# Query and key stacks with dimensions seven partitions apart, 112 contraction rows, rows of 8 KB and no memsets

## The chip, the cores and the metric

The kernel runs on one core of a Trainium2 chip. The metric is the device time of one execution in microseconds. The profile is one such execution.

## The reference, cut to what matters

Eight batches of `x` (256 channels by 512 positions) go through four layers: masked cross attention with 16 heads of 16 dimensions, a ternary-weight gated layer, a long convolution and an fp8 layer. The change touches the first one only:

```python
q = einsum('oc,bct->bot', Wq, layernorm(x)) + bq      # b, 256, 512
k = einsum('oc,bcs->bos', Wk, ctx) + bk
q, k, v = (t.reshape(b, 16, 16, 512) for t in (q, k, v))   # b, head, dim, position
dot = einsum('bhdt,bhds->bhts', q, k) / sqrt(16)
mask = target_mask[:, :, :, None] * source_mask[:, :, None, :]
dot = mask * dot - (1.0 - mask) * 1e6
amap = softmax(dot, axis=-1) * mask
out = einsum('bhts,bhds->bhdt', amap, v)
x = x + tanh(g_xattn[0]) * out
```

## The kernel before

**Projection** (`phase_project`, from about 0 to 133 us of the span). For each batch it computes q and k in fp32 and splits each into three bf16 parts (a value, the rest, the rest of that). They go to DRAM as `q_parts` and `k_parts`, shape (batch, part, 256 channels, 512). SyncE (SP) issues every DMA of the kernel, in program order; the three stores of a part tensor stand at L183. GpSimd also builds `rows8`, the mask rows, which SP stores once at L227 and L228 as `mask_q` and `mask_k`, 8 rows of 512 for each batch.

**Attention** (`phase_attention`, about 137 to 605 us) works on 16 units of 8 heads, two for each batch, u = 2b + h. For a unit SP fills one slot of `q_stack` and one of `k_stack` (four slots each, L530 and L536, in `load_unit`). A slot has 128 partitions by 8 heads by 512 positions of bf16. Its partitions are the contraction rows of a matmul. Six blocks of 16 partitions each hold the 16 dimensions of one part of q beside one part of k (`Q_PART`, `K_PART`), so that one bf16 matmul sums the six products that make an fp32-like score. Partitions 96 to 101 are mask rows and 102 and 103 hold the negated row maxima (`place_max`, L550, from `mrow`). Partitions 104 to 127 are zeroed once at the start (L621, L622 on GpSimd, L836, L837 on VectorE). In DRAM a head's 16 dimensions are adjacent channels, so a partition of a block, one dimension of 8 heads, is read as 8 rows of 1 KB.

The work on TensorE (PE) for each unit goes in 8 steps k. Each step has 4 score matmuls (L749, into `ps_s`), 4 matmuls for the maxima of later units (`max_tile`, L728, into `ps_m`, reduced by VectorE at L814) and 4 matmuls of probabilities with values (L759). ScalarE takes the exponentials (L696). The maxima run ahead: in steps 0 to 3 of unit u the second half of the tiles of unit u+1, from step 4 on the first half of unit u+2. Before that first tile of unit u+2 PE waits for all 14 DMAs of its slot (`qk_loaded`, L788). In step 4 PE also transposes the maxima (`turn_max`, L737), ScalarE copies them to `mrow` in step 5 (L674), and SP writes them into the stack (L550).

SP's order in a unit: `load_unit` for unit u+2 (14 DMAs), `gather_den` for unit u-1 (L565, L566 to DRAM, a wait until they have landed, L568 back, L571), in every other unit `load_batch`, `store_inv` (L577), `place_max` for u+1 (L550, waits for `mrow`), `spread_inv` (L583), weights (L545). Then the next unit's `load_unit`. The slot that it fills was freed long before, so its start is set by SP's order.

Of the kernel before, what the change touches and what calls it, by code (L numbers as in the profile page):

```python
# [6 lines left out]
BF16 = mybir.dt.bfloat16  # L7
# [4 lines left out]
P = 128  # L12
B = 8
C = 256
L = 512
CT = C // P
LT = L // P
ROWT = B * CT
HEADS, HD = 16, 16
UH = 8  # L20
# [7 lines left out]
BLOCKS = len(Q_PART)  # L28
MASK_ROW = BLOCKS * HD
MAX_ROW = MASK_ROW + BLOCKS  # L30
EXTRA = BLOCKS + 2


# [59 lines left out]
def phase_project(core, ctx, A):  # L93
# [4 lines left out]
    nc, X = core.nc, core.X  # L98
    RING = 3
    with ExitStack() as free:  # L100
# [9 lines left out]
        rows8 = sb("rows8", [B, 2, EXTRA, L], BF16)  # L110
# [7 lines left out]
        f = sb("qk_f", [P, 2, 2, CT, L], F32)  # L118
        r = sb("qk_r", [P, 2, 2, CT, L], F32)
# [12 lines left out]
        split_step, rows_ready, rows_stored = sem("split_step"), sem("rows_ready"), sem("rows_stored")  # L132
# [20 lines left out]
        with nc.Block() as block:  # L153

            @block.sync
            def _(sp):
# [59 lines left out]
                for b in range(B):  # L216
                    store_parts(b, KS)
                    if b + RING < B:
                        load_ctx(b + RING)
                    store_parts(b, QS)  # L220
                    if b + 2 < B:
                        load_mask(b + 2)
                        load_weights(b + 2)
                    store_values(b)
                    if b == 1:
                        sp.wait_ge(rows_ready, 2)
                        sp.dma_start(core.mask_q, rows8[:, 0]).then_inc(rows_stored, 16)  # L227
                        sp.dma_start(core.mask_k, rows8[:, 1]).then_inc(rows_stored, 16)  # L228
                sp.wait_ge(rows_stored, 32)
                for p in range(2):  # L230
# [219 lines left out]
def phase_attention(core, ctx, A):  # L450
# [6 lines left out]
    nc, X = core.nc, core.X  # L457
    DW = UH * L // P
    with ExitStack() as free:
# [13 lines left out]
        mrow = sb("mrow", [2 * UH, L], BF16)  # L473
# [5 lines left out]
        S = free.enter_context(nc.psum_tensor("ps_s", [P, 4, L], F32))  # L479
        M = free.enter_context(nc.psum_tensor("ps_m", [P, 3, L], F32))  # L480
# [5 lines left out]
        gate_ready, o_cleared = sem("gated_mask"), sem("o_cleared")  # L486
        zeroed = [sem(f"zeroed{i}") for i in range(4)]
# [22 lines left out]
        def bank(j):  # L510

            return (j if j < TURN_SLOT else j + 1) % 3
# [9 lines left out]
        with nc.Block() as block:  # L522

            @block.sync
            def _(sp):
                def load_unit(b, slot, h, fresh=False):
                    for blk in range(BLOCKS):
                        for dst, src, part in ((Q, core.q_parts, Q_PART[blk]), (K, core.k_parts, K_PART[blk])):
                            s = src[bass.ds(b, 1), part, h * P:(h + 1) * P, :]
                            sp.dma_start(dst[blk * HD:(blk + 1) * HD, slot],  # L530
                                         s.rearrange("a (h d) l -> d (a h) l", d=HD)).then_inc(qk_loaded[slot], 16)
                    if fresh:
                        sp.wait_ge(zeroed[slot], 2)
                    for dst, src in ((Q, core.mask_q), (K, core.mask_k)):
                        s = src[bass.ds(b, 1)].rearrange("a r l -> r a l").to_broadcast([EXTRA, UH, L])
                        sp.dma_start(dst[MASK_ROW:MASK_ROW + EXTRA, slot], s).then_inc(qk_loaded[slot], 16)  # L536

# [10 lines left out]
                def place_max(v, slot, h):  # L548
                    sp.wait_ge(mrow_ready, v + 1)
                    sp.dma_start(Q[MAX_ROW:MAX_ROW + 2, slot], mrow[:]).then_inc(m_placed[h], 16)  # L550

                load_unit(0, 0, 0, fresh=True)
                load_unit(0, 1, 1, fresh=True)
                load_batch(0, 0)
                load_weights(0, 0)
                load_weights(1, 1)
                sp.wait_ge(zeroed[2], 2)
                sp.wait_ge(zeroed[3], 2)
                place_max(0, 0, 0)
# [59 lines left out]
            def _(pool):  # L619
                for slot in (1, 3):  # L620
                    nc.gpsimd.memset(Q[96:P, slot], 0.0).then_inc(zeroed[slot], 1)  # L621
                    nc.gpsimd.memset(K[96:P, slot], 0.0).then_inc(zeroed[slot], 1)  # L622
                pool.wait_ge(zeroed[1], 2)
                pool.wait_ge(zeroed[3], 2)

                def batch(b, par, first, last):
# [90 lines left out]
            def _(pe):  # L717
                def max_tile(v, slot, tile, j):

                    hd, tc = tile // LT, tile % LT  # L720
                    n = TILES * v + tile
                    if j == TURN_SLOT + 2:
                        pe.wait_ge(mrow_ready, v)
                    elif TURN_SLOT <= j < TURN_SLOT + 2:
                        pe.wait_ge(max_red, n - 1)
                    elif not (same(v, 0) and tile < 3):
                        pe.wait_ge(max_red, n - 2)
                    nc.tensor.matmul(M[:, bank(j), :], Q[:, slot, hd, tc * P:(tc + 1) * P], K[:, slot, hd, :],  # L728
                                     start=True, stop=True).then_inc(max_mm, 1)
# [81 lines left out]
            def _(dve):  # L811
# [956 lines left out]
def build(nc, A, out):  # L1768
    core = Core()
# [5 lines left out]
    core.inv_rows = nc.dram_tensor("inv_rows", (2, UH, L), F32, kind="Internal").ap()  # L1775
    core.mask_q = nc.dram_tensor("mask_q", (B, EXTRA, L), BF16, kind="Internal").ap()
    core.mask_k = nc.dram_tensor("mask_k", (B, EXTRA, L), BF16, kind="Internal").ap()
    with ExitStack() as ctx:
# [10 lines left out]
        columns = sb("columns", [P, 16], F32)  # L1789
# [59 lines left out]
```

## Time and profile before

| | |
|---|---|
| median of 3 runs | 1348.16 us (1347.45 to 1355.43) |
| the profiled execution | 1347.74 us, span 1345.9 us |
| PE busy | 1115.3 us (83%) |
| VectorE busy | 1034.6 us (77%) |
| ScalarE busy | 667.1 us (50%) |
| GpSimd busy | 539.9 us (40%) |
| moved by DMA | 129.34 MB, mean 96 GB/s |
| attention, about 137 to 605 us | 468 us of the span |

The span is the profiled time from the first to the last instruction. PE is the busiest engine, but busy shares are means over four layers with different limits. What decides for this change is which wait ends last in the attention. The profile's own groups name it: the largest idle time ahead of the `ps_m` matmuls ends with a DMA into `k_stack`.

### The profile page before, as it was taken

Reading aid. Unit: us, or ns where it says so; the run is one execution under the profiler, and the core shown is the slowest. Engines: PE = TensorE matmul, PEld = TensorE weight load, DVE = VectorE, ACT = ScalarE, POOL = GpSimd, SP = SyncE. Lnnn points to the kernel's source line nnn. Section 1 sums busy time; section 2 is a strip of 40 time slices with the busy share of each in tenths; the row PEclk is TensorE's granted clock in tenths of the full one; section 3 lists DMA queues with packets and bytes.
Section 4 is the critical chain, followed back from the end, with each engine's and each line's share of the span. In section 5 each row is a group of like instructions: output and inputs, shape, how many; then the busy total and the mean of one; then the engine's idle time right before and its main releaser. Section 6 shows DMA issues by size and latency. Waiting matters only on the chain. (4 is left out here: it accounts for less than half of the span.)

```text
span 1345.9 us, 16068 instructions
## 1 busy us (share of the span) xinstructions
PE 1115.3 (83%) x4802; PEld 445.5 (33%) x4802; DVE 1034.6 (77%) x1564; ACT 667.1 (50%) x783; POOL 539.9 (40%) x407
## 2 busy tenths in 40 slices
PE   4985399978988899982899996699999999269676
PEld 2543022222222222211444443344444443134232
DVE  5787698866877787713999995588888887767898
ACT  1655057755767676781566664111000000486896
POOL 5766421423344234442011101587888886000021
PEclk8997679998999999996999999899999999589889
DMA  8798967765677656414111010111111110000011
GB/s 310 260 338 301 132 113 136 115 116 94 145 129 115 118 117 135 100 47 169 48 47 47 31 47 7 45 63 57 55 61 62 63 63 31 1 0 0 0 63 63
DMA packets 84275, 129.34 MB, mean 96 GB/s; under 512 B 13544, under 2 KB 53864, under 8 KB 83696
## 3 DMA queue, kind: packets, MB, share of 16 engines
q1 hardware_dynamic: 84224, 128.72, 39.2%
q8 instruction: 25, 0.41, 0.1%
q14 instruction: 26, 0.21, 0.1%
HBM read 104.44 MB, written 21.89 MB: 94 GB/s over the span
## 5 line engine op out<-in xcount | busy, mean ns | idle before, releaser
L814 DVE TENSOR_REDUCE mneg<-ps_m 128x1 f32<-128x512 f32 x512 | 321.9, 682 | 91.5 <-PE ps_m L728 90.8
L1358 PE MATMUL ps_y<-kv,toeplitz_sb 128*128 128x512 f32 x640 | 279.4, 595 | 10.0 <-POOL kv L1270 10.0
L696 ACT ACTIVATE probs<-ps_s 128x1024 f32<-128x1024 f32 x256 | 250.0, 1023 | 52.5 <-PE ps_s L749 52.3
L728 PE MATMUL ps_m<-k_stack,q_stack 128*128 128x512 bf16 x512 | 187.0, 406 | 59.3 <-DMA k_stack<-mask_k 55.3
L1358 PEld LDWEIGHTS ps_y<-kv,toeplitz_sb 128*128 128x128 f32 x640 | 121.0, 191 | 156.3 <-issue 156.3
L749 PE MATMUL ps_s<-q_stack,k_stack 128*128 128x512 bf16 x512 | 155.7, 388 | 11.7 <-ACT probs L696 11.2
L759 PE MATMUL ps_o<-probs,v_all 128*17 128x512 f32 x1024 | 139.5, 618 | 0.4 <-ACT probs L696 0.4
L1270 POOL TENSOR_TENSOR kv<-vT,ctxT_sb 128x2048 f32<-128x2048 f32 x32 | 118.7, 3710 | 39.1 <-PE ps_y L1358 32.4
L993 PE MATMUL ps_g<-w,xT_f 128*128 128x512 bf16 x512 | 120.1, 383 | 7.0 <-DVE h_f L1140 6.3
L644 POOL TENSOR_TENSOR inv_all<-inv_all,mb_b 128x512 f32<-128x512 f32 x16 | 20.4, 1274 | 252.2 <-DMA inv_all<-inv_rows 252.2
L1424 DVE TENSOR_TENSOR z<-ps_y,ctxT_sb 128x1024 f32<-128x1024 f32 x64 | 77.9, 1217 | 47.1 <-PE ps_y L1358 47.1
L728 PEld LDWEIGHTS ps_m<-k_stack,q_stack 128*128 128x128 bf16 x512 | 42.2, 99 | 217.0 <-DVE mneg L814 102.2
L1323 ACT ACTIVATE w_anchor<-w_f 128x512 f32<-128x512 f32 x32 | 20.1, 628 | 180.6 <-DMA w_f<-in_w 180.6
L1175 POOL TENSOR_TENSOR X<-X,down_sums 128x512 f32 (+1 forms) x16 | 20.5, 1283 | 195.6 <-ACT down_sums L1036 195.6
L1681 PE MATMUL ps_fp<-w 128*128 128x512 bf16 x256 | 66.3, 413 | 22.9 <-DVE w L1748 12.3
L1432 DVE TENSOR_REDUCE vT<-z 128x256 f32<-128x2304 f32 x32 | 81.7, 2553 | 1.1
L54 DVE BATCH_NORM_STATS2 bn<-X 128x6 f32<-128x512 f32 (+1 forms) x64 | 42.6, 683 | 46.9 <-POOL X L652 21.2
L749 PEld LDWEIGHTS ps_s<-q_stack,k_stack 128*128 128x128 bf16 x512 | 45.8, 98 | 81.6 <-ACT probs L696 34.3
L1048 ACT ACTIVATE sg_f<-ps_g,sc_f 128x512 f32<-128x512 f32 x64 | 42.7, 686 | 57.0 <-PE ps_g L993 37.7
L662 POOL TENSOR_SCALAR w<-w_sweep 128x512 bf16<-128x512 f32 x48 | 70.4, 1489 | 1.3
L993 PEld LDWEIGHTS ps_g<-w,xT_f 128*128 128x128 bf16 x512 | 48.4, 99 | 65.1 <-DVE h_f L1140 10.2
L980 PE MATMUL ps_d<-w,hT_f 128*128 128x512 bf16 x256 | 59.5, 387 | 1.6 <-ACT hT_f L1021 1.6
(163 smaller groups left out, 1649.7 us busy)
## 6 DMA issues: line engine op xcount, KB each, us to landing
w_sweep<-in_w SPq DMA_DIRECT2D x8, 1536.0 KB, 10.1
q_stack<-q_parts SPq DMA_DIRECT2D x96, 128.0 KB
k_stack<-k_parts SPq DMA_DIRECT2D x96, 128.0 KB
w_sweep<-in_w SPq DMA_DIRECT2D x16, 768.0 KB, 6.3
w_sweep<-in_w SPq DMA_DIRECT2D x16, 512.0 KB, 3.4
toeplitz_sb<-in_toeplitz SPq DMA_DIRECT2D x32, 256.0 KB, 2.6
w_f<-in_w SPq DMA_DIRECT2D x32, 256.0 KB, 2.9
k_parts<-qk_part SPq DMA_DIRECT2D x24, 256.0 KB, 7.5
```

The source lines that it names most:

```text
L662: nc.gpsimd.tensor_scalar(core.w3[:, m].rearrange("p a b -> p (a b)")[:, u * L:(u + 1) * L], wc[:, h, m, :], MAGIC, None, ALU.subtract).th ...
L696: nc.scalar.activation(pr[:, k % 2, 2 * slot:2 * slot + 2, :], S[:, 2 * slot:2 * slot + 2, :], ACT.Exp).then_inc(exp_done, 1)
L728: nc.tensor.matmul(M[:, bank(j), :], Q[:, slot, hd, tc * P:(tc + 1) * P], K[:, slot, hd, :], start=True, stop=True).then_inc(max_mm, 1)
L749: mm = nc.tensor.matmul(S[:, g, :], K[:, slot4, hd, (k % LT) * P:(k % LT + 1) * P], Q[:, slot4, hd, :], start=True, stop=True)
L759: mm = nc.tensor.matmul(O[32 * g:32 * g + HD + 1, :], V[:, par, sc, h * UH + 2 * g + G, :], pr[:, k % 2, g, :], start=(sc == 0), stop=(sc ...
L814: nc.vector.tensor_reduce(mneg[:, h, tile % LT, tile // LT:tile // LT + 1], M[:, bank(j), :], AX.X, ALU.max, negate=True).then_inc(max_red, 1)
L993: mm = nc.tensor.matmul(G[:, c % 2, j, :], xT[:, par, k, :], wt[:, k, c * L:(c + 1) * L], start=(k == 0), stop=(k == LT - 1))
L1270: nc.gpsimd.tensor_tensor(kv[:, g % 2].rearrange("p l (b j i) -> p (l b) j i", b=B, j=GROUP), over_j(group(vT, g)), over_i(group(cT, g)), ...
L1358: mm = nc.tensor.matmul(Y[:, q % 3, l2, :], T[:, g % 2, (lt - m) * P:(lt - m + 1) * P], kv[:, g % 2, m, :], start=(m == 0), stop=(m == lt))
L1424: nc.vector.tensor_tensor(z[:, g % 2, NB // 2 * half:NB // 2 * (half + 1), :, 0:GROUP], Y[:, q % 3].rearrange("p l (b j i) -> p (l b) j i" ...
L1432: nc.vector.tensor_reduce(group(vT, g), z[:, g % 2], AX.X, ALU.add).then_inc(red_ready, 1)
L1681: mm = nc.tensor.matmul(D[:, r, :], h8[:, j % 4, L * t + r * P:L * t + (r + 1) * P], proj[:, ot, :], start=(i == 0 and t == 0), stop=(i == ...
```

## The change

The partitions of a slot are laid out anew. Block j of dimension d stands at partition 7d + j instead of 16j + d, for j from 0 to 5, and partition 7d + 6 holds row d of the mask rows. That makes 112 rows (`ROWS`), all of them written by DMA, so the eight memsets and their semaphores go, and every matmul on the stacks reads partitions 0 to 111. The mask tensors in DRAM get 16 rows for each batch instead of 8. Rows 8 to 15 are written from the two constant rows of `rows8` (0 on the query side, 1 on the key side), so their products are 0. The maxima go to partitions 48 and 55. On the host the columns of `Wq` and `Wk` and both biases are permuted within each 128 channels from (head, dimension) to (dimension, head). A partition's 8 heads are then adjacent rows in DRAM and are read as one row of 8 KB. The order in which each engine issues is as before.

```diff
-MASK_ROW = BLOCKS * HD
-MAX_ROW = MASK_ROW + BLOCKS
+STEP = BLOCKS + 1
+ROWS = STEP * HD
 EXTRA = BLOCKS + 2
+MAX_ROW = STEP * BLOCKS + BLOCKS
...
-                        sp.dma_start(core.mask_q, rows8[:, 0]).then_inc(rows_stored, 16)
-                        sp.dma_start(core.mask_k, rows8[:, 1]).then_inc(rows_stored, 16)
+                        for side, dst in ((0, core.mask_q), (1, core.mask_k)):
+                            sp.dma_start(dst[:, 0:EXTRA], rows8[:, side]).then_inc(rows_stored, 16)
+                            for e in range(EXTRA, HD, 2):
+                                sp.dma_start(dst[:, e:e + 2], rows8[:, side, BLOCKS:EXTRA]).then_inc(rows_stored, 16)
...
-                            sp.dma_start(dst[blk * HD:(blk + 1) * HD, slot],
-                                         s.rearrange("a (h d) l -> d (a h) l", d=HD)).then_inc(qk_loaded[slot], 16)
-                    if fresh:
-                        sp.wait_ge(zeroed[slot], 2)
+                            sp.dma_start(dst[blk:ROWS:STEP, slot],
+                                         s.rearrange("a (d h) l -> d (a h) l", d=HD)).then_inc(qk_loaded[slot], 16)
                     for dst, src in ((Q, core.mask_q), (K, core.mask_k)):
-                        s = src[bass.ds(b, 1)].rearrange("a r l -> r a l").to_broadcast([EXTRA, UH, L])
-                        sp.dma_start(dst[MASK_ROW:MASK_ROW + EXTRA, slot], s).then_inc(qk_loaded[slot], 16)
+                        s = src[bass.ds(b, 1)].rearrange("a r l -> r a l").to_broadcast([HD, UH, L])
+                        sp.dma_start(dst[BLOCKS:ROWS:STEP, slot], s).then_inc(qk_loaded[slot], 16)
...
-                    sp.dma_start(Q[MAX_ROW:MAX_ROW + 2, slot], mrow[:]).then_inc(m_placed[h], 16)
+                    sp.dma_start(Q[MAX_ROW:MAX_ROW + STEP + 1:STEP, slot], mrow[:]).then_inc(m_placed[h], 16)
...
-                for slot in (1, 3):
-                    nc.gpsimd.memset(Q[96:P, slot], 0.0).then_inc(zeroed[slot], 1)
-                    nc.gpsimd.memset(K[96:P, slot], 0.0).then_inc(zeroed[slot], 1)
...
-                    nc.tensor.matmul(M[:, bank(j), :], Q[:, slot, hd, tc * P:(tc + 1) * P], K[:, slot, hd, :],
+                    nc.tensor.matmul(M[:, bank(j), :], Q[0:ROWS, slot, hd, tc * P:(tc + 1) * P],
+                                     K[0:ROWS, slot, hd, :],
...
-                        mm = nc.tensor.matmul(S[:, g, :], K[:, slot4, hd, (k % LT) * P:(k % LT + 1) * P],
-                                              Q[:, slot4, hd, :], start=True, stop=True)
+                        mm = nc.tensor.matmul(S[:, g, :], K[0:ROWS, slot4, hd, (k % LT) * P:(k % LT + 1) * P],
+                                              Q[0:ROWS, slot4, hd, :], start=True, stop=True)
...
-                for slot in (0, 2):
-                    nc.vector.memset(Q[96:P, slot], 0.0).then_inc(zeroed[slot], 1)
-                    nc.vector.memset(K[96:P, slot], 0.0).then_inc(zeroed[slot], 1)
...
+    def by_dim(v):
+        return np.ascontiguousarray(v.reshape(v.shape[:-1] + (CT, P // HD, HD)).swapaxes(-1, -2).reshape(v.shape))
```

SP at the end of one unit's load, before. The last number of a row is the shape that the DMA is issued with: partitions, rows for each, elements of a row.

```order
L530 DMA q_stack<-q_parts 16x8x512
L530 DMA k_stack<-k_parts 16x8x512
L536 DMA q_stack<-mask_q 8x8x512
L536 DMA k_stack<-mask_k 8x8x512
L539 DMA v_all<-v_rows 128x1088
```

The same place after the change.

```order
L532 DMA q_stack<-q_parts 16x4096
L532 DMA k_stack<-k_parts 16x4096
L536 DMA q_stack<-mask_q 16x8x512
L536 DMA k_stack<-mask_k 16x8x512
L539 DMA v_all<-v_rows 128x1088
```

A block's 8 rows of 512 elements for each partition have become one row of 4096 (8 KB). The mask rows stay rows of 1 KB and go to 16 partitions instead of 8. Nothing has changed places.

SP in the projection where the mask rows are stored, before.

```order
L189 DMA v_rows<-vp 128x1088 [waits v_ready]
L227 DMA mask_q<-rows 8x4096 [waits rows_ready]
L228 DMA mask_k<-rows 8x4096
L183 DMA k_parts<-qk_part 128x2x512 [waits p3_ready]
```

The same place after.

```order
L190 DMA v_rows<-vp 128x1088 [waits v_ready]
L229 DMA mask_q<-rows 8x4096 [waits rows_ready]
L231 DMA mask_q<-rows 8x1024 x4
L229 DMA mask_k<-rows 8x4096
L231 DMA mask_k<-rows 8x1024 x4
```

Eight small DMAs now stand between the values of batch 1 and the key parts of batch 2.

## Rows read from the trace of the kernel before

**Rows 1.** Waits in the attention: engine, line, releaser: us in total, times, longest.
```profile
PE ps_m L728 <- DMA k_stack<-mask_k: 55.3, 13, 21.7
PE ps_s L749 <- ACT probs L696: 11.2, 20, 1.1
PE ps_m L728 <- DVE mneg L814: 3.9, 15, 0.6
```

**Rows 2.** Timeline of the attention's start: start us, us, engine, instruction, idle before.
```profile
137.62 0.36 SPq L530 DMA_DIRECT2D q_stack<-q_parts  x1
142.28 0.43 SPq L530 DMA_DIRECT2D q_stack<-q_parts  x1
142.75 0.43 SPq L530 DMA_DIRECT2D k_stack<-k_parts  x1
140.25 1.76 DVE L837 MEMSET k_stack<- 32x2048 uint32 x1 [0.38 <-issue]
143.60 0.31 SPq L536 DMA_DIRECT2D k_stack<-mask_k  x1
154.12 2.00 PE L728 MATMUL ps_m<-k_stack,q_stack 128*128 128x512 bf16 x4 [21.65 <-DMA k_stack<-mask_k]
154.77 19.42 DVE L814 TENSOR_REDUCE mneg<-ps_m 128x1 f32<-128x512 f32 x32 [7.89 <-PE ps_m L728]
```

**Rows 3.** Busy time by stretch: A:B us, PE, PEld, DVE, ACT, POOL, PEclk, DMA share, GB/s.
```profile
148.50:154.10 5.60, 0.00 (x0) 0.00 (x0) 0.00 (x0) 0.00 (x0) 2.98 (x1) 0.50 1.13 128
258.50:265.00 6.50, 5.97 (x37) 1.69 (x34) 5.20 (x9) 5.90 (x8) 6.17 (x8) 1.00 1.13 125
160.00:166.00 6.00, 4.33 (x11) 0.97 (x11) 6.00 (x11) 0.00 (x0) 0.00 (x0) 0.91 1.13 117
40.00:70.00 30.00, 27.72 (x89) 16.45 (x87) 22.25 (x35) 20.74 (x31) 21.77 (x10) 1.00 0.90 303
```

**Rows 4.** DMA issues of the whole span: engine, count, KB each, median us to landing.
```profile
k_parts<-qk_part SPq DMA_DIRECT2D x24, 256.0 KB, 7.5
out<-X SPq DMA_DIRECT2D x16, 256.0 KB, 2.0
num<-odd_heads SPq DMA_DIRECT2D x64, 32.0 KB, 1.9
```

**Rows 5.** Timeline of PE at four units' first tiles, and the transposes behind two.
```profile
272.11 0.39 PE L728 MATMUL ps_m<-k_stack,q_stack 128*128 128x512 bf16 x1 [3.38 <-DMA k_stack<-mask_k]
302.35 0.61 PE L728 MATMUL ps_m<-k_stack,q_stack 128*128 128x512 bf16 x1 [6.29 <-DMA k_stack<-mask_k]
441.35 0.39 PE L728 MATMUL ps_m<-k_stack,q_stack 128*128 128x512 bf16 x1 [1.88 <-DMA k_stack<-mask_k]
443.83 0.39 PE L737 MATMUL ps_m<-ident,mm 128*16 128x128 bf16 x4
549.95 0.39 PE L728 MATMUL ps_m<-k_stack,q_stack 128*128 128x512 bf16 x1 [2.08 <-DMA k_stack<-mask_k]
554.02 0.39 PE L737 MATMUL ps_m<-ident,mm 128*16 128x128 bf16 x4
```

**Rows 6.** Busy time by stretch from one unit's first tile to the next's.
```profile
195.11:218.90 23.79, 23.25 (x133) 6.66 (x133) 20.45 (x34) 18.95 (x22) 4.78 (x4) 1.00 0.61 74
244.70:272.11 27.41, 23.48 (x133) 6.60 (x133) 21.28 (x36) 19.00 (x22) 11.05 (x10) 1.00 0.70 108
302.35:332.06 29.71, 25.82 (x132) 6.98 (x133) 21.42 (x36) 19.13 (x22) 11.05 (x10) 0.90 0.63 101
415.44:441.35 25.91, 23.48 (x133) 6.62 (x133) 21.28 (x36) 19.01 (x22) 11.05 (x10) 1.00 0.69 114
522.45:549.95 27.50, 24.88 (x133) 6.74 (x133) 21.26 (x36) 19.14 (x22) 11.06 (x10) 0.94 0.65 107
```

**Rows 7.** Timeline of SP in one unit.
```profile
259.38 0.54 SPq L565 DMA_DIRECT2D den_rows<-num  x1
272.35 0.36 SPq L568 DMA_DIRECT2D den<-den_rows  x1
277.09 0.70 SPq L550 DMA_DIRECT2D q_stack<-mrow  x1
282.33 0.33 SPq L530 DMA_DIRECT2D q_stack<-q_parts  x1
288.49 0.28 SPq L536 DMA_DIRECT2D k_stack<-mask_k  x1
```

**Rows 8.** Line 728: duration in ns min/median/max; then two score matmuls in the timeline.
```profile
L728 PEld LDWEIGHTS ps_m<-k_stack,q_stack x512: 95/98/152, 154.1 to 574.5; 128*128 128x128 bf16 x171
L728 PE MATMUL ps_m<-k_stack,q_stack x512: 379/379/634, 154.1 to 574.6; 128*128 128x512 bf16 x171
244.92 0.59 PE L749 MATMUL ps_s<-q_stack,k_stack 128*128 128x512 bf16 x2
```

**Rows 9.** Timeline of SP in the projection around the mask rows.
```profile
60.90 0.37 SPq L228 DMA_DIRECT2D mask_k<-rows  x1
62.09 1.82 SPq L183 DMA_DIRECT2D k_parts<-qk_part  x3
64.00 0.50 SPq L162 DMA_DIRECT2D cx<-in_ctx  x1
67.47 3.81 SPq L183 DMA_DIRECT2D q_parts<-qk_part  x3
```

More of the change, by code:

```diff
@@ L226, in _ @@
                         sp.wait_ge(rows_ready, 2)
-                        sp.dma_start(core.mask_q, rows8[:, 0]).then_inc(rows_stored, 16)
-                        sp.dma_start(core.mask_k, rows8[:, 1]).then_inc(rows_stored, 16)
-                sp.wait_ge(rows_stored, 32)
+                        for side, dst in ((0, core.mask_q), (1, core.mask_k)):
+                            sp.dma_start(dst[:, 0:EXTRA], rows8[:, side]).then_inc(rows_stored, 16)
+                            for e in range(EXTRA, HD, 2):
+                                sp.dma_start(dst[:, e:e + 2], rows8[:, side, BLOCKS:EXTRA]).then_inc(rows_stored, 16)
+                sp.wait_ge(rows_stored, 2 * 16 * (1 + (HD - EXTRA) // 2))
                 for p in range(2):
@@ L486, in phase_attention @@
         gate_ready, o_cleared = sem("gated_mask"), sem("o_cleared")
-        zeroed = [sem(f"zeroed{i}") for i in range(4)]
         qk_loaded = [sem(f"qk_loaded{i}") for i in range(4)]
@@ L525, in _, with load_unit @@
             def _(sp):
-                def load_unit(b, slot, h, fresh=False):
+                def load_unit(b, slot, h):
                     for blk in range(BLOCKS):
@@ L549, in place_max @@
                     sp.wait_ge(mrow_ready, v + 1)
-                    sp.dma_start(Q[MAX_ROW:MAX_ROW + 2, slot], mrow[:]).then_inc(m_placed[h], 16)
-                load_unit(0, 0, 0, fresh=True)
-                load_unit(0, 1, 1, fresh=True)
+                    sp.dma_start(Q[MAX_ROW:MAX_ROW + STEP + 1:STEP, slot], mrow[:]).then_inc(m_placed[h], 16)
+                load_unit(0, 0, 0)
+                load_unit(0, 1, 1)
                 load_batch(0, 0)
@@ L556, in _ @@
                 load_weights(1, 1)
-                sp.wait_ge(zeroed[2], 2)
-                sp.wait_ge(zeroed[3], 2)
                 place_max(0, 0, 0)
@@ L619, in _ @@
             def _(pool):
-                for slot in (1, 3):
-                    nc.gpsimd.memset(Q[96:P, slot], 0.0).then_inc(zeroed[slot], 1)
-                    nc.gpsimd.memset(K[96:P, slot], 0.0).then_inc(zeroed[slot], 1)
-                pool.wait_ge(zeroed[1], 2)
-                pool.wait_ge(zeroed[3], 2)
                 def batch(b, par, first, last):
@@ L1775, in build @@
     core.inv_rows = nc.dram_tensor("inv_rows", (2, UH, L), F32, kind="Internal").ap()
-    core.mask_q = nc.dram_tensor("mask_q", (B, EXTRA, L), BF16, kind="Internal").ap()
-    core.mask_k = nc.dram_tensor("mask_k", (B, EXTRA, L), BF16, kind="Internal").ap()
+    core.mask_q = nc.dram_tensor("mask_q", (B, HD, L), BF16, kind="Internal").ap()
+    core.mask_k = nc.dram_tensor("mask_k", (B, HD, L), BF16, kind="Internal").ap()
     with ExitStack() as ctx:
@@ L1830 @@
         "x": arr("x"), "ctx": arr("ctx_2048"), "mask": arr("mask_Bx1x2048_fk1"), "g_xattn": arr("g_xattn"),
-        "g_ffn": arr("g_ffn"), "bq": columns(inputs["L0_xattn_bq"]), "bk": columns(inputs["L0_xattn_bk"]),
+        "g_ffn": arr("g_ffn"), "bq": columns(by_dim(inputs["L0_xattn_bq"])), "bk": columns(by_dim(inputs["L0_xattn_bk"])),
         "mask_cols": np.ascontiguousarray(inputs["mask_Bx1x2048_fk1"].reshape(B, LT, P).transpose(2, 0, 1)),
         "bv": arr("L0_xattn_bv"),
-        "wqT": np.ascontiguousarray(inputs["L0_xattn_Wq"].T), "wkT": np.ascontiguousarray(inputs["L0_xattn_Wk"].T),
+        "wqT": by_dim(inputs["L0_xattn_Wq"].T), "wkT": by_dim(inputs["L0_xattn_Wk"].T),
         "wvT": np.ascontiguousarray(inputs["L0_xattn_Wv"].T),
```

## The prediction

> **What bounds the kernel now.** The list of waits, cut to the attention, comes first, because only the attention's loads change. PE's largest wait there is for the last DMA of a slot: 55.3 us in 13 waits, the longest 21.7 us [rows 1]. PE waits for ScalarE and VectorE 11.2 and 3.9 us. So the question is how long a unit's 14 load DMAs take, and what else hangs on them.
>
> The timeline of the start answers for the first unit. SP issues its first DMA at 137.62, the last (key mask rows) at 143.60 and is done with it at 143.91. PE starts at 154.12, 21.65 us idle, released by that load [rows 2]. The data is 10.2 us behind the issue. While it lands, the DMA engines show as fully busy but move only 128 GB/s; in a load inside the loop 125 GB/s; in the projection the same engines move 303 GB/s [rows 3]. A load is therefore limited by its own form. It has two features that the projection's traffic lacks: 16 adjacent partitions on the SBUF side, and rows of 1 KB on both sides. The rows alone are a weak reason: the projection's stores of `k_parts` are rows of 1 KB too (128x2x512), among the traffic at 303 GB/s.
>
> In the loop the same load ends PE's wait ahead of the first tile of unit u+2. Such waits are 3.38, 6.29, 1.88 and 2.08 us, for example [rows 5]; the 13 of the list less the first make 55.3 - 21.7 = 33.6 us. They cost more than that. The stretch from one unit's first tile to the next's is 27.41 us with a wait of 3.38 at its end, and 25.91 with 1.88: 24.03 us of work both times, at a granted clock of 1.00 [rows 5, 6]. But the stretch that begins behind the wait of 6.29 us has 0.90, and its PE work is 25.82 instead of 23.48 us [rows 6]: behind long waits the clock is at its lower level (1.2 of 2.4 GHz) for a few us.
>
> **The change part by part.**
>
> *Start.* One load is now 12 DMAs of 128 KB and 2 of 128 KB, 1.84 MB. At the 303 GB/s that the projection shows it would take 6.1 us; SP needs 143.91 - 137.62 = 6.3 us to issue it. I take the issue as the limit. Landing of the last one: about 2.3 us, beside 2.0 us for the stores of `out` (256 KB) and 1.9 for 32 KB, both in calm queues [rows 4]. PE starts at 143.9 + 2.3 = 146.2 instead of 154.12: **-7.9 us**. Everything behind it up to the loop is paced by VectorE's reductions (32 in 19.42 us [rows 2]) and moves along. The bounds are 0 (rate unchanged at 128 GB/s) and -10.2 (nothing behind the issue), some 1.5 us more if SP issues a DMA with fewer rows faster than the 0.47 us from one to the next [rows 2].
>
> The Trainium skill, SBUF — State Buffer, Door 1: The DMA port swizzle, says that the partition number decides which of 16 ports a transfer uses and that partitions 0 to 15 reach 4 of them, at about 104 GB/s; the trace agrees with its 125 to 128 GB/s, where two neighbouring loads overlap. By its formula partitions 7d + j reach 14 or 15 ports, none with more than two of the 16 rows. That rule would give 0.6 us for a DMA, 7.2 us for twelve, 0.9 us more than the issue, and the start would gain 7.0.
>
> *Loop.* From unit to unit the first tiles run from 195.11 to 549.95, 13 stretches in 354.84 us (first and last in [rows 6]). Without the load wait the first, 23.79 us, stays (it ends without one), and twelve take 24.03: 23.79 + 288.36 = 312.15. **-42.7 us**, of which some 33 are waits and some 9 clock. The clock's part rests on the stretches at 1.00, which have only short waits. After the last wait PE is slow once more: 554.02 - 549.95 = 4.07 us to the transposes against 443.83 - 441.35 = 2.48: **-1.6 us** [rows 5].
>
> This needs the load to be hidden in every unit. The worst case in the trace is the load whose first DMA was issued at 282.33 [rows 7]. PE wanted it at 302.35 - 6.29 = 296.06, 13.7 us later [rows 5]. The new load needs about 6.3 + 2.3 = 8.6, so 5.1 us of slack. It decides at (13.7 - 2.0) us for 1.84 MB, or 157 GB/s: above that no wait is left. The denominators profit too: they were issued at 259.38 behind the load and came back only at 272.35 [rows 7]; with the queues empty that is about 2 us instead of 12. So `place_max` will wait for `mrow` alone, and the next load starts no later than now relative to PE's steps.
>
> *Next limit.* With the loads away, PE is the bound at 23.48 of 24.03 us; VectorE has 21.28 and ScalarE 19.00 [rows 6].
>
> *Memsets.* Worth 0. VectorE's second one ends at 142.01, SP wants the mask rows of slot 0 only after 142.75 + 0.43 [rows 2]. Left in, they would still be hidden: the issue order is the same.
>
> *112 rows.* The number of columns is unchanged, and I take 0 for matmuls and weight loads. The trace has no matmul with fewer rows. See the third rival.
>
> *Mask rows.* Twice as many partitions, 8 rows of 1 KB each as before. I take them as 128 KB like a block in the 1.84 MB above. Its issue (0.31 us [rows 2]) may reach that of a block (0.43): 0.2 us at the start, within the landing estimate.
>
> *Projection.* SP has 8 more small DMAs of 16 KB, at 0.37 + 0.05 us each 3.4 us. SP is idle from 61.27 to 62.09 there and again from 64.50 to 67.47 [rows 9]. Key parts of batch 2 are stored 2.6 us later, the context of batch 5 is issued 2.6 us later, and the gap of 2.97 us ahead of the query parts takes it up. The 128 KB are 0.4 us at 303 GB/s in queues that are full. I take **+0.4**, bounds 0 and 3.4.
>
> **Sum.** -7.9 - 42.7 - 1.6 + 0.4 = -51.8 us. Against the profiled execution's 1347.74 that is 1296; the median of the runs, 1348.16, is 0.4 above it.
>
> **The rivals.**
>
> 1. *The load gets only somewhat faster* (chance 0.13), because 8 KB to a single partition, or DRAM, sets a rate between 128 and 157 GB/s, or because the mask rows land late. At 145 GB/s a load takes 12.7 + 2.0 = 14.7 us. The first unit starts at 137.62 + 14.7 = 152.3, 1.8 us earlier. In the worst units 1.0 us of wait is left, at most 12 us over all, so the loop gains 31 to 43: 1304 to 1316; nearer to 128 GB/s it reaches 1330. For it: each row still goes through one engine into one partition. Against it: the 303 GB/s that the same engines reach [rows 3].
>
> 2. *The loads are no faster* (0.07): their rate comes from something that both layouts share, such as 16 partitions for each DMA. Then the time stays near 1348, and the doubled mask bytes, 0.13 MB at 128 GB/s, add up to 1 us to each of 13 waits, 1361 at most. For it: the trace has no load of that size over spread partitions. Against it: fewer rows and more places to write leave no reason for the old rate that the rows show.
>
> 3. *112 rows make the weight load slow* (0.04), the case on the slower side. A weight load takes 98 ns and is hidden: two matmuls take 0.59 us, one 0.38, so they start 0.21 us apart [rows 8]. If fewer rows lost some fast form, nothing would show until the load exceeds 210 ns. Beyond that each ns counts for the 1,024 matmuls on the stacks: 50 ns more (260 ns in all) cost 51 us and eat the whole gain, 100 ns more cost 102 and give 1296 + 102 = 1398. The forecast turns into a loss from 260 ns on. The Trainium skill, TensorE: Matmul & The Clock Gate, Part 2, says that the load's time goes by columns and not by rows; no run here shows it yet, and by it this rival is void. A variant (0.02): the clock stays at its lower level because fewer rows count as less work. At 0.50 a unit's PE work nears twice 23.48 us, and 16 units make the time exceed 1600. Against it: at the start, with 11 matmuls in 6 us, the clock is already at 0.91 on average [rows 3].
>
> 4. *More than forecast* (0.04): issue and landing are both shorter and periods fall under 24.03 us, 1280 to 1286.
>
> **How the numbers follow.** Forecast 0.70 (1286 to 1304: the start's and the projection's bounds together). With the better half of rival 1, up to 1312, the range holds nearly 0.8. What a measurement of this kernel can tell from no change is 1%, 13.5 us. Faster by more: forecast 0.70, rival 1 0.13, rival 4 0.04, together 0.87. Within 1%: most of rival 2, 0.06. Slower: the rest of it, 0.01, and rival 3 with its variant, 0.06, together 0.07.
>
> **What would show it.** (a) PE's first `ps_m` matmul about 8.6 us behind SP's first stack DMA instead of 16.5. (b) No wait of PE on `k_stack` in the loop, all stretches from first tile to first tile near 24.0 us, granted clock 1.00. (c) About 10 us less between L565 and L568 on SP. (d) Weight loads of 98 ns and matmuls 0.21 us apart. (e) The projection's end within 0.5 us of now. It is wrong if stretches stay above 25 us, or if another wait stands where the load's did, such as for `mrow` in the stack.

## The result, and the profile after

The changed kernel takes 1309.63 us (median of 4 runs, 1308.91 to 1311.82), the kernel before 1349.37 in the same series (median of 4). The ratio is 0.970, interval 0.967 to 0.974: 39.7 us less, where 51.8 were forecast. The two profiled executions differ by 35.9 us (1347.74 and 1311.82; busy PE 1115.3 and 1114.2, moved 129.34 and 131.65 MB); the rest is the scatter of single executions. All accounts below are made between these two traces.

The page's row for the matmuls of the maxima, and the waits of the attention (137 to 605 us; total, times, longest). Line 720 is line 728 of before, 807 is 814.

```profile
L720 PE MATMUL ps_m<-k_stack,q_stack 112*128 112x512 bf16 x512 | 189.3, 410 | 26.9 <-DMA k_stack<-mask_k 16.1
```

```profile
PE ps_m L720 <- DMA k_stack<-mask_k: 16.1, 1, 16.1
DVE mneg L807 <- issue: 11.5, 4, 4.0
PE ps_m L720 <- DVE mneg L807: 10.8, 6, 3.3
```

Of the 13 waits for `k_stack` [rows 1] only the start's is left. One row is new: VectorE is idle for 11.5 us with nothing that the trace shows to wait for ("issue"). Another has grown: PE waits 10.8 us for the maxima, at most 3.3 at once, where it was 3.9 us, at most 0.6 [rows 1].

The start, from the timeline.

```profile
139.05 0.64 SPq L532 DMA_DIRECT2D q_stack<-q_parts  x1
139.75 0.57 SPq L532 DMA_DIRECT2D k_stack<-k_parts  x1
140.36 0.59 SPq L532 DMA_DIRECT2D q_stack<-q_parts  x1
...
147.36 0.60 SPq L536 DMA_DIRECT2D k_stack<-mask_k  x1
149.99 1.03 PE L720 MATMUL ps_m<-k_stack,q_stack 112*128 112x512 bf16 x2 [16.07 <-DMA k_stack<-mask_k]
```

PE starts 2.0 us behind the last issue's end (147.96), where it took 10.2 [rows 2]. But SP now needs 0.63 us from one issue to the next instead of 0.47, so the 14 of them need 8.9 us instead of 6.3.

Busy time by stretch (A:B us, PE, PEld, DVE, ACT, POOL, PEclk, DMA share, GB/s): five us in which only stack loads move, then four units, each from its transposes to the next unit's.

```profile
143.00:148.00 5.00, 0.00 (x0) 0.00 (x0) 0.00 (x0) 0.00 (x0) 0.00 (x0) 0.50 0.69 210
```

```profile
290.27:314.16 23.89, 23.20 (x132) 6.80 (x133) 20.96 (x37) 19.14 (x23) 11.05 (x10) 1.00 0.53 164
314.16:345.45 31.29, 26.09 (x132) 7.26 (x132) 21.19 (x37) 19.35 (x23) 10.04 (x9) 0.89 0.34 99
393.14:417.03 23.89, 23.20 (x133) 6.80 (x133) 20.96 (x37) 19.14 (x23) 11.05 (x10) 1.00 0.54 164
417.03:447.93 30.90, 26.02 (x133) 7.25 (x133) 21.19 (x37) 19.35 (x23) 10.05 (x9) 0.89 0.33 101
```

The rate is 210 GB/s where it was 128 [rows 3]. The DMA engines are busy for 0.69 of that time, and 128 KB every 0.63 us would be 208 GB/s, an estimate from the issues above. So SP's issue sets the rate here and no longer the load's form.

The units of the loop take 23.8 to 23.9 us at a clock of 1.00, as forecast, except two. Those two lose 31.29 + 30.90 - 2 x 23.89 = 14.4 us. They lie four units apart: units 2 to 13 run as a hardware loop of 3 iterations of 4 units, and the two places are its two turns. The timeline of VectorE and PE at the first turn:

```profile
328.24 0.69 DVE L807 TENSOR_REDUCE mneg<-ps_m 128x1 f32<-128x512 f32 x1 [4.03 <-issue]
328.99 0.39 PE L720 MATMUL ps_m<-k_stack,q_stack 112*128 112x512 bf16 x1 [3.28 <-DVE mneg L807]
330.82 2.48 DVE L807 TENSOR_REDUCE mneg<-ps_m 128x1 f32<-128x512 f32 x4 [1.89 <-issue]
331.57 0.61 PE L720 MATMUL ps_m<-k_stack,q_stack 112*128 112x512 bf16 x1 [1.76 <-DVE mneg L807]
331.97 1.06 PE L742 MATMUL ps_s<-q_stack,k_stack 112*128 112x512 bf16 x2
333.39 1.91 PE L752 MATMUL ps_o<-probs,v_all 128*17 128x512 f32 x8
```

VectorE stands still for 4.03 and 1.89 us, PE's next maxima matmul waits for it, and behind the pause PE runs at its lower clock level: the same 8 matmuls of line 752 take 1.05 us elsewhere (last fence of this section) and 1.91 here. So 5.9 us of standing still cost the unit 31.29 - 23.89 = 7.4 us.

The DMA view, attention only, has one more difference, on the queue named "instruction" (queue: packets, MB, share). Before:

```profile
q14 instruction: 10, 0.08, 0.1%
```

After:

```profile
q14 instruction: 20, 0.16, 0.1%
```

In the 15 us around the first turn, 320 to 335, the changed kernel has three packets of this queue:

```profile
q14 instruction: 3, 0.02, 0.6%
```

One of them is moved between 325 and 328 us, inside VectorE's first pause (324.2 to 328.2), and one between 328 and 331, which holds the second (328.9 to 330.8).

Other rows that answer to those of before. The denominators of one unit on SP (line 566 was 568), and the last matmul of the attention, which stood at 604.77:

```profile
233.36 0.58 SPq L563 DMA_DIRECT2D den_rows<-num  x1
233.98 0.55 SPq L564 DMA_DIRECT2D den_rows<-odd_heads  x1
235.72 0.33 SPq L566 DMA_DIRECT2D den<-den_rows  x1
```

```profile
568.76 1.05 PE L752 MATMUL ps_o<-probs,v_all 128*17 128x512 f32 x8
570.17 1.05 PE L752 MATMUL ps_o<-probs,v_all 128*17 128x512 f32 x8 [0.36 <-ACT probs L688]
```

### The profile page after: what moved, and what is told of

It is laid out like the page before. It is cut to its first block and busy times, and to the rows that moved or that the text cites. A ratio compares the mean times of both kernels' runs of the same rounds, so it can differ in the third digit from the quotient of the medians.

```text
span 1310.0 us, 16066 instructions
## 1 busy us (share of the span) xinstructions
PE 1114.2 (85%) x4802; PEld 449.6 (34%) x4802; DVE 1020.2 (78%) x1560; ACT 668.9 (51%) x783; POOL 525.9 (40%) x403
## 2 busy tenths in 40 slices
DMA packets 65213, 131.65 MB, mean 100 GB/s; under 512 B 13864, under 2 KB 31656, under 8 KB 61552
## 5 line engine op out<-in xcount | busy, mean ns | idle before, releaser
L720 PE MATMUL ps_m<-k_stack,q_stack 112*128 112x512 bf16 x512 | 189.3, 410 | 26.9 <-DMA k_stack<-mask_k 16.1
L742 PE MATMUL ps_s<-q_stack,k_stack 112*128 112x512 bf16 x512 | 155.2, 387 | 10.4 <-ACT probs L688 10.1
L752 PE MATMUL ps_o<-probs,v_all 128*17 128x512 f32 x1024 | 136.5, 605 | 0.4 <-ACT probs L688 0.4
L720 PEld LDWEIGHTS ps_m<-k_stack,q_stack 112*128 112x128 bf16 x512 | 43.5, 99 | 182.4 <-DVE mneg L807 99.1
L742 PEld LDWEIGHTS ps_s<-q_stack,k_stack 112*128 112x128 bf16 x512 | 46.6, 99 | 79.7 <-ACT probs L688 30.7
L1038 ACT ACTIVATE sg_f<-ps_g,sc_f 128x512 f32<-128x512 f32 x64 | 42.7, 686 | 57.1 <-PE ps_g L983 37.7
```

The costliest lines, as they stand in the source:

```text
L720: nc.tensor.matmul(M[:, bank(j), :], Q[0:ROWS, slot, hd, tc * P:(tc + 1) * P], K[0:ROWS, slot, hd, :], start=True, stop=True).then_inc(max ...
L742: mm = nc.tensor.matmul(S[:, g, :], K[0:ROWS, slot4, hd, (k % LT) * P:(k % LT + 1) * P], Q[0:ROWS, slot4, hd, :], start=True, stop=True)
L752: mm = nc.tensor.matmul(O[32 * g:32 * g + HD + 1, :], V[:, par, sc, h * UH + 2 * g + G, :], pr[:, k % 2, g, :], start=(sc == 0), stop=(sc ...
```

## Theories

The forecast treats placement (partitions 7 apart) and row size (8 KB) as one thing. Theory A: the rate comes from placement alone. Rival: from the longer rows. On the stalls, Theory F: at a loop's turn VectorE must fetch its instructions again, and whether it must depends on where the loop lies in its program, which the four missing memsets moved. Rivals: the 8 KB rows hold up that fetch; or the stall belongs to the new layout in some other way. The expectations give letters to these and other cases, and say beside each what it holds: B is row size as the cause of the rate; C, E and G are other causes of the stalls than the one under test; D is the first form of F, a fetch at the turn that the stack loads delay.

Every series had the kernel before in it, and each ratio is against that series: median 1352.66 us beside rows1, adj8, rows4 and unroll8, 1349.30 beside pad4, pad2, step2 and stores4, 1353.02 beside step2_m2, before_m2 and pad4_stores4. Differences in us between kernels of different series carry that scatter.

## Experiments on placement and row size

**rows1**: the changed kernel's partitions, the old rows of 1 KB. The host permutation goes.

```diff
-                            sp.dma_start(dst[blk:ROWS:STEP, slot],
-                                         s.rearrange("a (d h) l -> d (a h) l", d=HD)).then_inc(qk_loaded[slot], 16)
+                            sp.dma_start(dst[blk:ROWS:STEP, slot].rearrange("p (e r) l -> p e (r l)", r=1),
+                                         s.rearrange("a (e d r) l -> d (a e) (r l)", d=HD, r=1))
```

> The changed kernel with the host permutation and the load's source as before, so that every partition of a block is again read as 8 rows of 1 KB, while the partitions stay 7 apart. Theory A (16 adjacent partitions limit the old load, not the rows): the load stays fast; PE starts the attention within 1 us of the changed kernel's distance from SP's first stack DMA (10.9 us) or sooner, the loop keeps stretches of 23.9 us and no wait on the stack. SP issues a DMA each 0.47 us again (before: 0.47, changed kernel: 0.63). If the two stalls of 7 us at the loop's turns come from 8 KB rows ahead of instruction fetches, they vanish and the time is 1295 to 1300. Rival B (the rows of 1 KB limit it): the load moves 108 to 128 GB/s as before, the waits on the stack return, and the time is 1340 to 1350. Rival C (the stalls come from the new timing and not from the rows): fast load but stalls as in the changed kernel, 1307 to 1311.

Measured: 1308.42 us, 0.968 (0.962 to 0.974), as fast as the changed kernel. SP's issues are again 0.60 us long, PE starts 11.0 us behind the first. The two turns take 29.06 and 29.48 us. Rows of 1 KB are not what made the old loads slow. The stalls were to vanish if the 8 KB rows made them; they stayed, as rival C says.

**adj8**: the kernel before with the host permutation, so adjacent partitions and rows of 8 KB.

```diff
-                                         s.rearrange("a (h d) l -> d (a h) l", d=HD)).then_inc(qk_loaded[slot], 16)
+                                         s.rearrange("a (d h) l -> d (a h) l", d=HD)).then_inc(qk_loaded[slot], 16)
```

> The kernel before with only the host permutation and the load's source changed: rows of 8 KB to 16 adjacent partitions, memsets, 128 contraction rows and the mask rows as before. Theory A (adjacent partitions limit the load): the rate stays near 108 to 128 GB/s, the waits on the stack stay, 1340 to 1355. Rival B (row size): the loop's waits go, 1300 to 1315. SP's time for one issue tells whether 0.63 us belongs to the rows of 8 KB (then 0.63 here too) or to partitions that are not adjacent (then 0.47 here).

Measured: 1354.56 us, 1.002 (0.999 to 1.005). Its waits, the start of its SP timeline, and the stretch in which its first load lands:

```profile
PE ps_m L728 <- DMA k_stack<-mask_k: 59.2, 14, 22.4
```

```profile
138.42 0.41 SPq L530 DMA_DIRECT2D k_stack<-k_parts  x1
138.88 0.41 SPq L530 DMA_DIRECT2D q_stack<-q_parts  x1
```

```profile
148.50:154.10 5.60, 0.00 (x0) 0.00 (x0) 0.00 (x0) 0.00 (x0) 3.38 (x1) 0.50 1.04 117
```

8 KB rows into 16 adjacent partitions move 117 GB/s, no more than the 128 of before [rows 3]. And SP needs 0.46 us from one issue to the next: the longer issue belongs to the spread partitions, not to the rows. Both halves of the pair say the same, so Theory A stands.

**rows4**: rows of 4 KB, partitions 7 apart (in rows1's diff r is 4).

> The changed kernel with rows of 4 KB, two for each partition of a block (heads 0 to 3 and 4 to 7 apart in DRAM). If the stalls at the loop's turns grow with the row size, they are 7 us each in the changed kernel, 0 at 1 KB and between at 4 KB (about 3 us each), and the time is 1300 to 1306. If they depend on the timing alone they stay at 7 us: 1307 to 1311. SP's issue: 0.63 us if the number of rows has no part in it, less if it does.

Measured: 1308.49 us, 0.968 (0.962 to 0.974); the turns take 30.09 and 30.36 us. Over 1, 4 and 8 KB the stalls at a turn are 5.4, 6.3 and 7.2 us (means of two, over 23.89). But stores4 below has rows of 8 KB too, and its turns take 30.35 and 30.32 us, 6.4 over. Row size does not make the stalls; whether it changes their length, one trace for each kernel does not show.

**step2**: one edit of the kernel before. Blocks j and j+1 are interleaved over 32 partitions, each block on every second one; rows of 1 KB, 128 contraction rows and all memsets stay.

```diff
-                            sp.dma_start(dst[blk * HD:(blk + 1) * HD, slot],
+                            at = 2 * HD * (blk // 2) + blk % 2
+                            sp.dma_start(dst[at:at + 2 * HD:2, slot],
```

> The kernel before with one edit in the load: blocks j and j+1 share 32 partitions, every second one each (partitions 32 * (j // 2) + j % 2 + 2d), rows of 1 KB, memsets, 128 contraction rows, mask rows of 8 partitions and weights unpermuted as before. By the port rule such a block reaches 8 ports, and the load is limited by SP's issue (0.47 to 0.63 us for each DMA). Then the waits on the stack in the loop vanish or nearly so (the loads need more than 157 GB/s for that). Since VectorE's program is as before, theory F expects no stall at the loop's turns and thus 1294 to 1300, better than the changed kernel; rival G expects stalls and 1306 to 1311. If only a spread over the whole height helps, the waits stay and the time is 1340 to 1350.

Measured: 1295.87 us, 0.961 (0.957 to 0.966), 13.8 us less than the whole change. From its windows, its DMA view and its timeline:

```profile
138.00:143.00 5.00, 0.00 (x0) 0.00 (x0) 4.25 (x3) 0.00 (x0) 5.00 (x2) 0.50 0.65 206
```

```profile
q14 instruction: 10, 0.08, 0.1%
```

```profile
134.33 0.74 SPq L531 DMA_DIRECT2D q_stack<-q_parts  x1
...
142.72 0.31 SPq L537 DMA_DIRECT2D k_stack<-mask_k  x1
...
146.86 1.03 PE L729 MATMUL ps_m<-k_stack,q_stack 128*128 128x512 bf16 x2 [17.66 <-DMA k_stack<-mask_k]
```

Every second partition already gives 206 GB/s, again the rate of SP's issue, with the engines busy for 0.65 of the time. The start is 12.5 us behind the first issue, 1.6 more than 7 apart. SP's issues are done at 143.03, so it is the landing that takes 3.8 us instead of 2.0; that its mask rows still go to 8 adjacent partitions may be the reason, and was not tried. But no wait is left in the loop, there is no stall, and the mask stores are the old two. So 112 rows, 8 KB and a step of 7 are all unneeded for the loop; and the gain is larger where VectorE's program is left as it was.

## Experiments on the two stalls

**unroll8**: the changed kernel with the attention's hardware loop written out.

```diff
-            with eng.Fori(0, (B - 2) // 2) as i:
+            for i in range((B - 2) // 2):
```

> The changed kernel with the attention's hardware loop of three iterations written out for all engines; the same instructions in the same order, with no branch in the attention. Theory D (the two stalls of 7 us are instruction fetches at the loop's back-edge, late behind the stack loads): both vanish, each unit takes 23.9 us, and the time falls by 14 us to 1295. Rival E (something else at that place, such as a semaphore or a DMA of the kernel): the stalls stay and so does 1309.

Measured: 1298.39 us, 0.960 (0.954 to 0.966), 11.2 us less than the changed kernel where 14 were expected. The units at both places take 23.9 us and VectorE's "issue" row is gone. The instruction queue has 15 packets in the attention, whose program is now written out at full length, but none from 320 to 335. The stalls need the loop's turn.

**pad4**: the changed kernel with four memsets of one column of a spare tile on VectorE, where the four memsets of the stacks stood. They compute nothing.

```diff
+        spare = sb("spare", [P, 4], F32)
...
+                for i in range(4):
+                    nc.vector.memset(spare[:, i:i + 1], 0.0)
                 nc.vector.memset(O[:], 0.0).then_inc(o_cleared, 1)
```

> The changed kernel with four memsets of one column of a spare tile on VectorE where the four memsets of the stacks stood, so that VectorE's loop begins as many instructions into its program as in the kernel before. Everything else, also the timing of the loads, is as in the changed kernel. Theory F (the two stalls of 7 us are extra instruction fetches of VectorE, which the position of its loop in the program decides): no idle time of VectorE without a releaser at the loop's turns, about 10 instead of 20 packets on the small instruction queue in the attention, every unit 23.9 us, 1296 to 1299. Rival G (VectorE fetches at every turn in any layout, and the new timing only exposes it): stalls and packets as in the changed kernel, 1308 to 1311.

Measured: 1296.94 us, 0.962 (0.958 to 0.967), 12.7 us under the changed kernel. Three units over the first turn, and the packets:

```profile
288.50:312.38 23.88, 23.20 (x132) 6.79 (x132) 20.93 (x37) 19.14 (x23) 11.06 (x10) 1.00 0.57 164
312.38:336.27 23.89, 23.20 (x133) 6.79 (x133) 20.94 (x37) 19.15 (x23) 10.05 (x9) 1.00 0.43 129
336.27:360.15 23.88, 23.20 (x132) 6.79 (x132) 20.94 (x37) 19.14 (x23) 11.05 (x10) 1.00 0.54 163
```

```profile
q14 instruction: 11, 0.09, 0.1%
```

The unit over the turn takes 23.89 us instead of 31.29, and the packets are 11 instead of 20, with none from 320 to 335. Same layout, same rows: four instructions that do nothing take the stalls away.

**pad2**: the same with two.

> As pad4 with two memsets instead of four. Theory F: either as pad4 or as the changed kernel, nothing between (about 10 or 20 packets; 1297 or 1309). Rival G: 1309.

Measured (one run): 1312.86 us.

```profile
DVE mneg L808 <- issue: 12.8, 2, 6.5
```

```profile
q14 instruction: 20, 0.16, 0.1%
```

Two do not help; the pause changes its form (one of 6.5 us a turn instead of two, of 4.0 and 1.9).

**step2_m2**: the reversal. step2, with VectorE's four memsets written as two that clear the same bytes. SP's wait for the memsets of slot 2 goes too, so SP's program is one wait shorter.

```diff
-                sp.wait_ge(zeroed[2], 2)
...
-                for slot in (0, 2):
-                    nc.vector.memset(Q[96:P, slot], 0.0).then_inc(zeroed[slot], 1)
-                    nc.vector.memset(K[96:P, slot], 0.0).then_inc(zeroed[slot], 1)
+                nc.vector.memset(Q[96:P, 0:3:2], 0.0).then_inc(zeroed[0], 1)
+                nc.vector.memset(K[96:P, 0:3:2], 0.0).then_inc(zeroed[0], 1)
```

> The kernel step2 (median 1295.9, no stalls at the loop's turns, 10 packets on the small instruction queue in the attention) with VectorE's four memsets of the stacks as two, each over the slots 0 and 2 together: the same bytes, two instructions fewer in front of VectorE's loop, the position at which pad2 stalls. Theory F (position decides): VectorE is idle without a releaser for some us at both turns, about 20 packets, 1306 to 1311. Rival G (112 rows, the missing memsets or the DMAs of the changed kernel bring the stalls, not the position): 1294 to 1299 and 10 packets.

Measured: 1314.79 us, 0.973 (0.970 to 0.976), 18.9 us over step2 as the medians stand, 16 us by the two ratios. PE starts 12.5 us behind SP's first issue as in step2, and the turns take 32.58 and 32.42 us where step2 has 23.9.

```profile
DVE mneg L814 <- issue: 15.8, 2, 8.5
```

```profile
q14 instruction: 19, 0.16, 0.1%
```

The stall appears in a kernel without partitions 7 apart, without 8 KB rows and with 128 rows. The rivals that tie it to those parts of the change fall. Spread partitions are left, and the next run takes them away.

**before_m2**: the same edit on the kernel before, with SP's wait taken out too.

> The kernel before with the same edit: VectorE's loop two instructions earlier, loads slow as before. Theory F: the stalls and the 20 packets come here too. A unit's load is timed from SP's order and not from PE, so where PE waits for the load anyway (1.8 to 6.3 us in each unit) most of a stall is hidden behind it, and the time rises by 2 to 8 us. If the median does not rise and there are 20 packets, the slow loads hide the stall completely; 10 packets would go against the theory.

Measured: 1374.02 us, 1.018 (1.015 to 1.022), 21 us over the kernel before. The stall comes with the old layout too. It was expected to be partly hidden in the waits for the slow loads, at 2 to 8 us more. Hardly any of it was. The start adds little: PE begins 17.2 us behind SP's first issue, 0.7 more than before. Its VectorE at the first turn, and that unit:

```profile
358.27 2.48 DVE L813 TENSOR_REDUCE mneg<-ps_m 128x1 f32<-128x512 f32 x4 [16.05 <-issue]
```

```profile
331.96:372.19 40.23, 24.73 (x133) 7.21 (x132) 21.18 (x37) 19.46 (x24) 10.03 (x9) 0.83 0.50 96
```

The same unit takes 25.83 us in the kernel before (336.02 to 361.85). The packets are 19 (before 10), two of them inside this pause. The pause is 16.05 us at this turn and 14.48 at the other, instead of 4.1 to 8.5 in the kernels with fast loads: it is longest where the stacks' loads are slow and keep the queues full, and that was missing in the expectation. This fits a fetch that shares the DMA engines with the data. No run took the fetch apart from the loads, so this part is a reading, not shown.

## Experiments on the projection's stores

**stores4**: the changed kernel with the eight small stores as two.

```diff
-                            for e in range(EXTRA, HD, 2):
-                                sp.dma_start(dst[:, e:e + 2], rows8[:, side, BLOCKS:EXTRA]).then_inc(rows_stored, 16)
+                            two = rows8[:, side, BLOCKS:EXTRA].rearrange("b e l -> b (e l)").unsqueeze(1)
+                            sp.dma_start(dst[:, EXTRA:HD].rearrange("b (r e) l -> b r (e l)", e=2),
+                                         two.to_broadcast([B, 4, 2 * L])).then_inc(rows_stored, 16)
```

> The changed kernel with the four small stores of the constant rows on each side as one DMA, so 4 instead of 10 DMAs for the mask tensors. SP's first stack DMA is 1.4 us later in the changed kernel than before (139.05 against 137.62). If those stores are the cause, it comes about 1 us earlier and the time falls to 1308 to 1309; if they are not, nothing changes (139.0, 1309.6).

Measured: 1307.77 us, 0.971 (0.966 to 0.975). SP's first stack DMA moves from 139.05 to 136.44 us, but the time moves by no more than its scatter: the same DMA stands at 137.62 before, 138.02 in adj8 and 134.33 in step2, three kernels with the same two stores. Over all kernels, though, the DMA stands at 138.39 to 139.68 in the six with all ten stores and at 134.33 to 138.02 in the five with two, on average 2.7 us apart and without overlap. So the stores do delay SP. How much of that the time pays is not shown: the medians differ by 1.9 us. The turns take 30.35 and 30.32 us, so the loop's stalls stay.

**pad4_stores4**: both repairs.

> The changed kernel with both repairs: four spare memsets on VectorE (pad4, 1296.9 alone) and 4 instead of 10 DMAs for the mask tensors (stores4, 1307.8 against 1309.6). If the two add, 1295; if the stores' part was noise, 1297.

Measured: 1295.98 us (median of 5), 0.959 (0.956 to 0.961). The interval overlaps those of pad4, step2 and unroll8. These four are the best versions, and no run here separates them; step2 is the smallest edit of the kernel before.

## Why the prediction was right or wrong

Forecast 1296, measured 1309.63: inside the range, but by luck. The forecast's own case was 1286 to 1304; up to 1312 the range was widened for the better half of rival 1, a load that gets only somewhat faster, and that did not happen. The bounds named for the forecast's own case also add up otherwise: the start's and the projection's give 1292 to 1307, not 1286 to 1304, and the measured time is outside either. The gain fell 12 to 16 us short of the forecast's. Between the two traces 15.9 us of the 51.8 are missing:

| step | forecast | measured |
|---|---|---|
| projection's end (first stack DMA) | +0.4 | +1.4 |
| first DMA to PE's start | -7.9 | -5.6 |
| unit 0, clock | 0 | +1.3 |
| loop, to the last unit's transposes | -44.3 | -31.8 |
| later layers | 0 | -1.3 |
| sum (from unrounded terms) | -51.8 | -35.9 |

*The rate of a load: right.* PE's waits in the loop are gone, and the landing of the last DMA is 2.0 us. The forecast put the cause on adjacent partitions and called 1 KB rows "a weak reason"; rows1 and adj8 show that with both signs. The Trainium skill, SBUF — State Buffer, Door 1: The DMA port swizzle, ties the rate to the ports that the partition numbers reach, and has 104 GB/s for partitions 0 to 15; the trace has 117 to 128 GB/s for 16 adjacent ones. The 206 and 210 GB/s of the spread ones are SP's issue rate, so they show only that the new limit lies higher. Rivals 1 and 2 did not happen.

*Start: a term mis-sized.* "SP needs 143.91 - 137.62 = 6.3 us to issue it" took the issue's duration from rows of the old layout, and the bounds allowed only a faster issue. The time of an issue depends on the layout too: 0.63 us from one to the next for 7 apart, 0.64 for 2 apart, 0.46 to 0.47 for adjacent. The 14 issues take 8.9 - 6.3 = 2.6 us more, less 0.3 for a landing of 2.0 instead of 2.3: the whole miss of check (a), 10.9 us instead of 8.6. The text had named this as the limit of the start, so the term deserved a bound on its upper side. In the loop the longer issue is hidden: 10.9 us for a load are less than the 13.7 that it has.

*Clock after the start: not in the sum.* Before, PE's clock had reached 0.66 on average from its start to unit 0's transposes; after, it is 0.50 throughout that stretch of the same 21.9 us. Unit 0 then takes 23.09 us instead of 21.77. This is not a mark of the new layout as such: with the same partitions rows4 and stores4 take 21.89 us for unit 0, pad4 22.12 and rows1 22.99. What makes the clock rise earlier or later was not tried. The later units are at 1.00, as forecast.

*Loop: the mechanism right, one step failed.* From unit 1's transposes to the last unit's the trace has 347.2 us (194.93 to 542.12) against 379.0 (197.75 to 576.71): the -31.8 of the table, beside -42.7 and -1.6 of the forecast. Without the two turns the loop gained 31.8 + 14.4 = 46.2 us, 1.9 more than forecast, since units take 23.8 to 23.9 us and not 24.03. The failed step is "Memsets. Worth 0 ... Left in, they would still be hidden: the issue order is the same". As work they were hidden. But they were also four instructions ahead of VectorE's loop, and taking them out moved the loop within its program. Since then each of the two turns costs VectorE two pauses, 4.0 and 1.9 us at the first, and the unit 7.0 to 7.4. Shown from both sides: with four dummies in the memsets' place the stalls go and 12.7 us come back (pad4); with the memsets halved in two kernels that had no stalls, they come (step2_m2, before_m2). That the turn is the place shows in unroll8. That the pause is a fetch of instructions rests on the releaser "issue" and on the packets of the queue named "instruction", 19 or 20 in the attention of all seven stalling kernels, 10 or 11 in the five others that keep the loop, and 15 in unroll8. From 320 to 335 us, around the first turn, the six stalling kernels with fast loads have three each, and step2, pad4, pad4_stores4 and unroll8 none. The trace does not say which engine a packet is for. The Trainium skill, Runtime: NRT & Kernel Launch, Instruction fetch mechanics, says that a taken branch whose target isn't at hand forces a DMA fetch before execution goes on; the trace agrees, with those packets and with 5.9 and 5.6 us in which VectorE stands still at the two turns. Which boundary decides is open: in the changed kernel 0 and 2 instructions stall (2 in a single run), 4 do not, and no run placed the loop elsewhere.

*Denominators, 112 rows: right.* From line 564's issue to line 566's are 1.7 us and from 563's 2.4, where the round trip took 13.0 [rows 7]. By form, the weight loads of line 720 last 95/98/152 ns and its matmuls 379/379/634 with 112 rows:

```profile
L720 PEld LDWEIGHTS ps_m<-k_stack,q_stack x512: 95/98/152, 150.0 to 539.9; 112*128 112x128 bf16 x171
L720 PE MATMUL ps_m<-k_stack,q_stack x512: 379/379/634, 150.0 to 540.0; 112*128 112x512 bf16 x171
```

Those are the numbers of [rows 8] for 128 rows, so rival 3 is void, and by the same row step2's 128 rows are as good as 112.

*Projection: +0.4 against +1.4.* The gap on SP took up only part of the stores. The four small ones of a side took 1.57 and 1.39 us, and behind them the key parts' three issues took 3.38 us where they took 1.82 [rows 9]:

```profile
60.13 1.57 SPq L231 DMA_DIRECT2D mask_q<-rows  x4
61.74 0.29 SPq L229 DMA_DIRECT2D mask_k<-rows  x1
62.07 1.39 SPq L231 DMA_DIRECT2D mask_k<-rows  x4
63.51 3.38 SPq L184 DMA_DIRECT2D k_parts<-qk_part  x3
66.99 3.65 SPq L163 DMA_DIRECT2D cx<-in_ctx  x1
```

The +1.4 lies inside the bounds 0 to 3.4. The same point over all kernels (under stores4) makes it 2.7 on average, so the forecast's +0.4 was small for SP.

Of the five checks, (b) failed at two of the units, (a) by 2.3 us, (e) by 0.9; (c) and (d) held. The closing sentence named "another wait stands where the load's did, such as for `mrow`" as a sign of error; one came, but from an engine's own program.

## What to carry to other kernels

For DMAs of 16 partitions, look at which partitions they write before looking at row length: here an interleave of two blocks, two lines of code, gave the whole loop's gain, and longer rows gave nothing. Price the issue time of a DMA in its new form when the queue that issues it is on the path. When an edit adds or removes instructions ahead of a hardware loop, even hidden ones, look in the new trace for idle time put down to "issue" at the loop's turns and for the instruction queue's packet count, and compare with a version padded to the old count before crediting or blaming the edit itself.

## What was not expected of the hardware

- SP's issue of a 128 KB DMA takes 0.63 to 0.64 us from one to the next when the 16 partitions are 2 or 7 apart, and 0.46 to 0.47 when they are adjacent, at any row size tried (1, 4, 8 KB spread; 1, 8 KB adjacent).
- Two to four VectorE instructions ahead of a hardware loop decide 13 to 21 us: each of its two turns costs VectorE nothing, or 4.1 us (rows1) to 8.5 us (step2_m2) with fast loads, or 14.5 to 16 us where slow loads fill the queues (before_m2).
- The changed kernel's pauses of 5.9 and 5.6 us cost 7.4 and 7.0 us, because PE runs for a few us at its lower clock level behind them (8 matmuls in 1.91 us instead of 1.05).
